# One order of TensorE's work changed in the latents' attention: four heads' logits in one go ahead of the turns

## What is computed

```python
h = jnp.concatenate([x, latents], axis=1)            # 375 context rows and 112 latents
q = (latents @ q_w + q_b).reshape(b, k_len, NH, DH)  # 16 heads of 32
kv = (h @ kv_w + kv_b).reshape(b, p + k_len, NH, DH, 2)
kmat, v = (kv[..., 0], kv[..., 1])
attn = jnp.einsum('bkhd,bnhd->bhkn', q, kmat) / DH
attn = jnp.where(full_mask[:, None, None, :], attn, -jnp.inf)
attn = jax.nn.softmax(attn.astype(jnp.float32), axis=-1).astype(q.dtype)
attn_out = jnp.einsum('bhkn,bnhd->bkhd', attn, v).reshape(b, k_len, H)
attn_out = attn_out @ out_w + out_b + residual
```

## Time and profile before

| | |
|---|---|
| median of 3 runs | 3185.2 us (3182.51 to 3185.8) |
| profiled execution | 3191.91 us, span of the core 3190.6 us |
| TensorE matmuls, busy | 3032.4 us, 95% of the span |
| TensorE weight loads | 2550.8 us, 80% |
| VectorE / ScalarE / GpSimd busy | 1341.4 / 1117.8 / 1005.1 us (42 / 35 / 32%) |
| mean granted TensorE clock | 0.969 of full speed |
| DMA, mean | 91 GB/s |

### The profile page before, as it was taken

The page is one execution under the profiler, slowest core; times in us unless marked ns, Lnnn a source line. Parts: engine busy times, 40 slices in busy tenths (PEclk is TensorE's granted clock), DMA queues, the critical chain, the costliest instruction groups (busy, mean ns, idle before and its releaser), DMA issues.

```text
span 3190.6 us, 43414 instructions
## 1 busy us (share of the span) xinstructions
PE 3032.4 (95%) x16412; PEld 2550.8 (80%) x16412; DVE 1341.4 (42%) x3085; ACT 1117.8 (35%) x2541; POOL 1005.1 (32%) x932
## 2 busy tenths in 40 slices
PE   6898888899999999999999999999989999998999
PEld 2564556788998998888989989989878877777887
DVE  4785786433332333433333333333421155563134
ACT  2333334443222223333232222323333355554332
POOL 4554563322112113222121121221244233345421
PEclk8898899999999999999999999999999999998999
DMA  6554651533112122112222221221111211101133
GB/s 215 177 181 162 187 173 43 176 128 110 72 72 99 46 73 104 63 69 84 75 92 72 72 92 72 72 86 58 53 54 53 67 42 44 42 28 67 53 104 101
DMA packets 98117, 289.74 MB, mean 91 GB/s; under 512 B 8408, under 2 KB 55000, under 8 KB 89080
## 3 DMA queue, kind: packets, MB, share of 16 engines
q1 hardware_dynamic: 97432, 286.27, 26.3%
q10 hardware_dynamic: 480, 0.69, 0.1%
HBM read 262.94 MB, written 23.99 MB: 90 GB/s over the span
## 4 chain that ended last, share of the span: by engine, by line
PE 77%; DVE 6%; POOL 6%; ACT 5%; issue 3%; DMA 2%; PEldq 0%; PEld 0%; SPq 0%; POOLq 0%; ACTq 0%; DVEq 0%
PE bank L189 21%; PE bank L190 20%; PE bank L191 20%; PE bank L1849 5%; POOL W_lo L229 3%; PE bank L1834 2%; PE bank L2467 2%; DMA W_raw<-in_weights 2%; PE bank L651 1%; DVE max L2059 1%; ACT prob L1937 1%; ACT W_hi L220 1%; PE bank L2481 1%; DMA v_spread<-v_rows 1%; POOL y L1267 1%
## 5 line engine op out<-in xcount | busy, mean ns | idle before, releaser
L2143 POOL TENSOR_SCALAR prob<-prob,inverse 112x376 f32<-112x376 f32 x256 | 144.3, 585 | 1275.0 <-DVE inverse L2065 1275.0
L229 POOL TENSOR_TENSOR W_lo<-W_raw,W_hi 128x1024 fp32r<-128x1024 f32 x138 | 329.5, 2410 | 161.8 <-ACT W_hi L220 158.3
L189 PE MATMUL bank<-ctx_hi,W_hi 128*128 128x376 f32 x1024 | 353.8, 345 | 6.2 <-DVE K_lo L271 3.6
L271 DVE SCALAR_TENSOR_TENSOR K_lo<-bank,vectors,K_hi 128x375 fp32r<-128x375 f32 (+1 forms) x288 | 172.8, 606 | 410.8 <-ACT K_hi L262 410.8
L190 PE MATMUL bank<-ctx_lo,W_hi 128*128 128x376 f32 x1024 | 343.6, 336 | 0.0
L191 PE MATMUL bank<-ctx_hi,W_lo 128*128 128x376 f32 x1024 | 343.4, 335 | 0.0
L189 PE MATMUL bank<-act_hi,W_hi 128*128 128x448 f32 x784 | 313.8, 400 | 10.1 <-DVE act_lo L269 3.6
L2010 DVE TENSOR_TENSOR V<-bank,bv 128x512 f32<-128x512 f32 x168 | 116.3, 692 | 433.5 <-PE bank L1849 235.5
L1937 ACT ACTIVATE prob<-bank,minus 112x376 f32<-112x376 f32 x256 | 143.7, 573 | 434.3 <-DVE minus L2062 434.3
L190 PE MATMUL bank<-act_lo,W_hi 128*128 128x448 f32 x784 | 293.2, 374 | 0.0
L191 PE MATMUL bank<-act_hi,W_lo 128*128 128x448 f32 x784 | 292.2, 373 | 0.0
(11 more groups left out here) (269 smaller groups left out, 6287.6 us busy)
## 6 DMA issues: line engine op xcount, KB each, us to landing
W_raw<-in_weights SPq DMA_DIRECT2D x69, 1024.0 KB, 4.9
ctx_hi<-ctx_split SPq DMA_DIRECT2D x64, 752.0 KB, 4.3
ctx_lo<-ctx_split SPq DMA_DIRECT2D x64, 752.0 KB, 5.8
v_spread<-v_rows SPq DMA_DIRECT2D x128, 224.0 KB
att<-in_ctxT SPq DMA_DIRECT2D x16, 376.0 KB, 5.3
ctx_split<-W_hi SPq DMA_DIRECT2D x16, 376.0 KB, 3.8
ctx_split<-W_lo SPq DMA_DIRECT2D x16, 376.0 KB, 4.9
W_hi<-ctx_split SPq DMA_DIRECT2D x32, 188.0 KB, 4.0
```

Source lines behind the costliest of these rows:

```text
L189: nc.tensor.matmul(dst, left[0], right[0], start=first, stop=False)
L229: pool.tensor_tensor(k.Wl[:, slot, cs, :], k.Wraw[:, cs, :], k.Wh[:, slot, cs, :].bitcast(F32), ALU.subtract).then_inc(*k.w_low.now((n, i)))
L271: dve.scalar_tensor_tensor(out=low, in0=src, scalar=bias, in1=high.bitcast(F32), op0=ALU.add, op1=ALU.subtract).then_inc(*k.banks.draining ...
L2143: pool.tensor_scalar(k.Pm[:, h, :], k.Pm[:, h, :], k.rsum[:, h:h + 1], 1.0, ALU.mult, ALU.mult).then_inc(*k.prob_done.now((n, h)))
```

## The change

A function `logits_first` rewrites the list of a batch, and `pe_latents`, TensorE's walk, uses the rewritten list. `plan_latents` and the walks of the other engines still use `logit_steps(b)`, so banks, drains and softmaxes keep their order.

```diff
+def logits_first(steps):
+
+    out = []
+    for step in steps:
+        if step[0] != "logits":
+            out.append(step)
+        elif 0 in step[3]:
+            at = len(out) - 1 if out and out[-1][0] == "turns" else len(out)
+            out.insert(at, step[0:3] + ((0, 1, 2, 3),))
+    return out
+
 def plan_latents(k):
@@ pe_latents
     for b in range(B):
-        for what, *which in logit_steps(b):
+        for what, *which in logits_first(logit_steps(b)):
             if what == "logits":
                 pe_logits2(k, *which)
```

## The result

The changed kernel takes 3162.9 us (median of 4 runs, 3158.59 to 3168.03) against 3185.05 us: a ratio of 0.9933, 95% interval 0.9918 to 0.9947. A second set of five runs of the same kernel gave 0.9923 (0.9911 to 0.9936). The forecast was 3163.5 us.

A forecast was written before the change was run, and what follows sets the result against it. TensorE's own sequence was taken to bound batches 0 to 6. Batches 0, 1 (5.0), 2 to 6 (10.9) and 7 (2.7) give 18.6 us, plus 3.1 for the clock: 21.7 off 3185.2, so 3163.5 us; range 3158 to 3174.

The forecast's parts named there:

- The packing: Logits in each step: four heads' 12 matmuls together take 0.87 us, hardly more than the six of a pair.
- it doesn't pack: Rival: behind values, four heads take the time of two pairs, 1.72 us; about 4 us gain left, 3181; chance 0.05.
- The step: Every step on TensorE: logits 0.87 plus 16 transposes 1.83; 0.81 us less a step, 19.4 us for 24.
- Attend 0: o = 0, batches from 2 on: TensorE newly waits 0.5 us for VectorE's copy 3.
- Turns of o = 2: Next turn 2 after o = 1, batches from 2 on: new wait for act_lo, 0.3 us at most, taken as 0.25.
- Turns 3: No logits ahead, less cover: new wait 0.4 us in batches 0, 1; 0.25 in 2, 4, 5, 6; none in 3.
- The wait at the turns of o = 1: Batches from 2 on: the present wait for K_lo ahead of these turns goes, counted as 0.7 us gained.
- Batches 0 and 1: Logits stand in TensorE's idle time at o = 0; with the other steps and waits 2.5 us gained each, 5.0 together.
- Batch 7: Goes by the chain: 1.9 us until GpSimd's weight split limits, plus an estimated 0.8 next step; 2.7 together.
- The clock in batch 1: Idle time falls from 1.4 to some 0.5 us, so the clock stays up: 3.1 us more gain.
- The rival of the other engines: Their chain is 1 us longer than counted, each step loses 0.5 us: gain 9.7, 3175.5 us; chance 0.13.
- the three signs of being wrong: TensorE waits over 3 us each in batches 2 to 6, four-head group longer behind values than attend, or new clock falls.

The follow-up runs named there:

- apart: Changed kernel with both logits pairs still ahead of the turns, but separated by the values or projection, so no burst of four: 3181.6 us, ratio 0.9988 to before.
- between: Changed kernel with the four-head logits burst kept whole but placed between turns (0,1) and turns (2,3): 3166.8 us, ratio 0.9931 to before.
- norm: Changed kernel with VectorE's second projection addition and moments moved into softmax gaps, scaling and GpSimd's root moved later: 3163.8 us, ratio 0.9935 to before.
- actorder: Changed kernel with ScalarE's scaled copies of normed rows moved behind attend 1 and their high halves behind its copies of turns 2: 3155.5 us, ratio 0.9911 to before.
- terms: Changed kernel with the burst's 12 matmuls queued by product and not by head: 3161.0 us, ratio 0.9919 to before.

## Why the prediction was right, point by point

- **The packing.** Predicted 0.87 us for the four heads behind values as behind an attend; it is 0.86 or 0.87 in every place of batches 2 to 6, so the rival that it doesn't pack is out. apart and between show that the gain is this and not the order. A tail that grows with the heads is 0.02 us at most, 0.87 us for four against 0.85 for two, and not the 60 ns of the estimate.
- **The turns were mis-sized.** The step was forecast at 0.81 us less, from 1.83 us for 16 transposes. It is 1.03 less (2599.09 to 2607.62 in batch 1, 8.53 in place of 9.56), because the transposes take 1.52; against these 0.31 us, values take up to 0.1 longer when logits and not turns follow them. The 1.83 had a wait in it. TensorE's weight loads show it, in the kernel before at the turns that rows 3 took the number from, and in the changed one at the same place of batch 2:

```profile
2667.87 1.48 PEld L2467 LDWEIGHTS bank<-ident,prob 112*128 112x128 f32 x15
2669.67 0.19 PEld L189 LDWEIGHTS bank<-W_hi 128*128 128x128 f32 x1 [0.32 <-issue]
```
```profile
2655.49 0.33 PEld L2478 LDWEIGHTS bank<-ident,prob 112*128 112x128 f32 x3
2656.13 1.15 PEld L2478 LDWEIGHTS bank<-ident,prob 112*128 112x128 f32 x12 [0.32 <-POOL prob L2774]
```

  In the first the loads of the turns end at 2669.35 and those of the keys follow 0.32 us later, put down to no one; the keys use the bank of turn 0, which ScalarE was then copying. In the second the second turn waits 0.32 us, while K_lo is being made. A group that stands next to a wait had been taken for its bare cost. So 0.2 us a step, some 5 us in 24 places, was missing from the gain.
- **The new waits were at the places named, and two of them longer.** Attend 0: 0.5 predicted, 0.9 measured (keys to attend 3.14 us in place of 2.25). Turns of o = 2: 0.25 predicted, 0.6 measured (2.13 us in place of 1.52). Turns 3 of batches 0 and 1 wait 0.7 us (2.25 us), but 0.3 of that is the wait that the 1.83 hid before: the 0.4 predicted as new is right. Turns 3 of batches 2, 4, 5 and 6 take 1.83 as before; the 0.25 predicted for them didn't come. The chains of the other engines ran as counted: the first exponential comes 5.49 us after the logits of its step (2642.95 against 2637.46; 5.47 predicted) and the second half of the turns of o = 2 starts at 11.24 (2648.70; 11.22 predicted). The waits grew because TensorE reaches these places some 0.3 us earlier than in the sum. At attend 0 something is added: the sum let it start 0.14 us after the end of copy 3, a figure read at a turn, and it starts 0.36 us after it (2633.60 against 2632.62 + 0.62). norm shows which of VectorE's work the first wait stands behind, and actorder that taking ScalarE's away ends the second and lets another come. That the sum fits is in part luck: the gain without waits was too small and the waits were too small, and the two errors largely offset each other. A batch 6 of 39.1 us was forecast, and it is 38.99.
- **The wait at the turns of o = 1 is gone**, as said: in batch 2 these turns are the 16 of 2638.33, in 1.52 us. That it had been K_lo's bank and not GpSimd's product, as the profile names it, the trace of the kernel before bears out: head 1's product had ended at 2647.04, and the bank's semaphore, which TensorE's queue passes at 2648.63 just ahead of the turn at 2648.69, is the one that K_lo raises at its end, 2648.54.
- **Batches 0 and 1**: 2.5 us each predicted without the clock, 3.06 measured in batch 0. **Batch 3**: 2.4 predicted, 2.1 measured.
- **Batch 7**: 2.7 predicted, 2.66 measured, and by the chain named: in the trace the first exponential of o = 1 comes 12.99 us after the start of the batch (12.95 before), and GpSimd's products of o = 2 at 21.76 in place of 23.68, right behind the split.
- **The clock in batch 1** stays up, as forecast, and 3.1 of the 21.7 us are this term. The reason given, a shorter idle time, isn't borne out: between kept its clock with 1.36 us of idle time, and apart lost it with 0.83. So the term came true on a reason that the runs don't support, which is luck.
- **Sum**: 21.7 us predicted; 23.1 in the batches of the profile, 22.2 between the medians. The rival of the other engines is there in part: TensorE's waits are 6.2 us longer in all, and 13.2 of the 15.6 us are now for VectorE. It is what the Trainium skill says in "TensorEngine Tiling (Array Packing)", section "PSUM Bottleneck", that packing speeds up TensorE but not the draining of PSUM, and the trace agrees, but with 6.2 us against a gain of 23.1. None of the three signs of being wrong came: TensorE's waits in batch 2, for one, add up to less than 2 us.

## What to carry to other kernels

In this kernel matmuls of 32 rows (three of 488 columns a head) cost by the burst and not by the matmul: two heads took 0.85 us and four 0.87, so it pays to bring together what uses different row groups even where nothing waits for it. When a duration is taken from a timeline as the price of a moved group, look at the weight loads for a gap inside or behind it; a short wait hides in a group as well as in a listed idle time. And a faster engine meets its suppliers at new places: the two waits that grew most in a batch of the bulk were for drains behind unrelated work, and an edit that cures it in the bulk of the loop must be looked at in the last iteration, where the cover is missing.

## What the runs showed of the hardware that was not expected

- TensorE doesn't start matmuls in the order of its queue when they use different row groups, other than the text ahead of the prediction has it of every engine. In the changed kernel the queue has head 0's three products, then head 1's, and the first products of all four heads start within 0.03 us from 2637.46 on, 0.3 us before any second product; with the queue sorted by product (terms) the burst is 0.84 us in place of 0.87.
- The clock's fall in batch 1 came in both profiles of the kernel before (3.1 and 4.6 us, behind waits of 1.36 and 1.41 us) and in batch 0, with the same kind of work and a wait of 1.41 us, in neither. In apart it came behind a wait of 0.83 us, and in between not behind one of 1.36.
